# Four buffers for the feature-major context and a one-pair-at-a-time order on TensorE in a cross-attention layer

## What is computed

```
x = x + _L2_xattn_ref(_layernorm(x, axis=-1), ctx_1024, ctx_1024, mask_BxSxS2_ff0, Wq, Wk, Wv)

def _L2_xattn_ref(x1, x2, x3, mask, Wq, Wk, Wv):
    q = einsum('bsd,hd->bsh', x1, Wq)        # 8 x 64 x 256
    k = einsum('bsd,hd->bsh', x2, Wk)        # 8 x 1601 x 256
    v = einsum('bsd,hd->bsh', x3, Wv)
    scores = einsum('bqh,bkh->bqk', q, k) / sqrt(256)
    weights = softmax(scores + mask, axis=-1)
    return einsum('bqk,bkh->bqh', weights, v)
```

## Time and profile before

| | us |
|---|---|
| median of 3 runs | 3238.86 (3234.41 to 3239.84) |
| the profiled execution, its own time | 3242.19 |
| span of the profiled execution | 3240.4 |
| TensorE busy / VectorE busy / ScalarE busy | 2822.7 / 1634.3 / 1088.7 |
| this layer's first instruction, start | 2382.4 |
| first and last `scores`, start | 2397.8 and 2480.7 |
| last `mix`, start | 2502.8 |
| next layer's first instruction, start | 2519.4 |

### The profile page before, as it was taken

One profiled execution on the slowest core, in us unless ns is written; L12 is line 12 of the kernel. 1 busy time (PEld: TensorE's weight loads), 2 busy tenths in 40 slices (PEclk: granted clock), 3 DMA queues, 4 the chain that ended last, 5 costly groups with the idle time before them and its releaser, 6 DMA issues. The chain is left out here.

```text
span 3240.4 us, 43628 instructions
## 1 busy us (share of the span) xinstructions
PE 2822.7 (87%) x17456; PEld 1910.0 (59%) x17456; DVE 1634.3 (50%) x3626; ACT 1088.7 (34%) x1925; POOL 522.3 (16%) x280
## 2 busy tenths in 40 slices
PE   5899999999999998789999779989955789588776
PEld 2566666666666665446565536657932559477644
DVE  5556565665646454445555357754520520355463
ACT  2333333333333331135555446622311613111120
POOL 2012020211202000000000007731010320243200
PEclk8899999999999999889999989999977889799888
DMA  4123323232322210311000001126856158332101
GB/s 139 45 53 73 69 55 66 54 66 54 66 59 61 54 44 23 145 45 42 21 21 22 1 16 40 43 84 243 301 191 203 50 193 306 131 122 82 32 1 33
DMA packets 92096, 271.40 MB, mean 84 GB/s; under 512 B 7920, under 2 KB 57096, under 8 KB 85240
## 3 DMA queue, kind: packets, MB, share of 16 engines
q1 hardware_dynamic: 87896, 259.65, 26.6%
q0 software_dynamic: 2976, 8.13, 0.7%
q10 hardware_dynamic: 1024, 0.86, 0.1%
HBM read 256.64 MB, written 11.44 MB: 83 GB/s over the span
## 5 line engine op out<-in xcount | busy, mean ns | idle before, releaser
L1375 PE MATMUL L_xattn_bank<-L_xattn_keys_tok,L_xattn_probsT 119*128 119x257 f32 (+1 forms) x1792 | 452.7, 393 | 9.3 <-ACT L_xattn_probsT L1211 0.4
L1312 PE MATMUL L_xattn_wide<-L_xattn_keys_feat,weights_a 128*128 128x512 f32 (+2 forms) x1024 | 386.4, 521 | 1.3 <-DVE L_xattn_k_rnorm L1024 0.7
L1375 PEld LDWEIGHTS L_xattn_bank<-L_xattn_keys_tok,L_xattn_probsT 119*128 119x128 f32 (+1 forms) x1792 | 320.9, 190 | 96.5 <-issue 33.1
L1312 PEld LDWEIGHTS L_xattn_wide<-L_xattn_keys_feat,weights_a 128*128 128x128 f32 x1024 | 192.0, 193 | 153.8 <-issue 127.7
L1020 DVE COPY L_xattn_k_normed<-L_xattn_wide 128x833 f32<-128x833 f32 (+1 forms) x128 | 131.3, 1026 | 231.2 <-PE L_xattn_wide L1312 231.2
L2315 DVE TENSOR_TENSOR_SCAN L_attn_state<-L_attn_decay,L_attn_banks 128x1024 f32<-128x1024 f32 x80 | 182.7, 2286 | 69.6 <-PE L_attn_banks L2518 61.6
L1590 DVE CUSTOM_DVE_ANT_0 L_xattn_scores<-L_xattn_banks,L_xattn_mask 128x512 f32<-128x512 f32 (+1 forms) x256 | 131.4, 570 | 151.8 <-issue 151.8
L2421 POOL TENSOR_TENSOR L_attn_state<-L_attn_state,L_attn_C_rows 128x1024 f32<-128x1024 f32 x80 | 188.7, 2360 | 70.3 <-DVE L_attn_state L2315 70.2
L1126 POOL TENSOR_TENSOR L_xattn_keys_tok<-L_xattn_keys_tok,weights_a 119x1792 f32<-119x1792 f32 (+2 forms) x24 | 61.1, 2546 | 856.1 <-DVE L_xattn_keys_tok L965 856.1
L1205 ACT ACTIVATE L_xattn_scores<-L_xattn_scores,L_xattn_neg_max 128x833 f32<-128x833 f32 x128 | 119.6, 982 | 208.6 <-DVE L_xattn_neg_max L1045 208.6
L2518 PEld LDWEIGHTS L_attn_banks<-L_attn_B_diagonal,L_attn_dt_u_tok 128*128 128x128 f32 x1280 | 150.4, 193 | 66.3 <-issue 64.7
(11 more groups left out here) (504 smaller groups left out, 4562.6 us busy)
## 6 DMA issues: line engine op xcount, KB each, us to landing
L_xattn_k_scale<-L_xattn_k_scale_rows SPq DMA_DIRECT2D x128, 417.0 KB, 5.1
L_xattn_ctx_feat<-in_ctx_feat SPq DMA_DIRECT2D x24, 1601.0 KB, 10.0
L_ffn_expert_w<-in_x_L_ffn SPq DMA_DIRECT2D x16, 2056.0 KB, 8.0
L_ffn_expert_w<-in_x_L_ffn SPq DMA_DIRECT2D x15, 1028.0 KB, 6.2
L_ffn_expert_w<-in_x_L_ffn SPq DMA_DIRECT2D x15, 1024.0 KB, 5.2
L_attn_C_rows<-L_attn_c_rows SPq DMA_DIRECT2D x48, 256.0 KB, 3.2
L_xattn_ctx_tok<-in_ctx_tok SPq DMA_DIRECT2D x8, 1536.0 KB
L_xattn_ctx_tok_and_one<-in_ctx_tok SPq DMA_DIRECT2D x8, 1536.0 KB
```

What stands on the lines that cost most here:

```text
L1312: last = nc.tensor.matmul(wide[:, 2 * h + c, 0:n], wk[:, k, p * P:(p + 1) * P], xnT[b % 2][:, k, a:a + n], start=(k == 0), stop=(k == KT - 1))
L1375: last = nc.tensor.matmul(bS[:, 0:D + 1], pT[0:r, c, a, :, :].rearrange("p h q -> p (h q)"), xn[b % 2][0:r, t, :], start=(i == 0), stop=(i ...
```

## The change

Three edits, all in `l2_xattn`. The features get four buffers instead of three (`FEAT = 4`), and the waits of their loads are counted by four; the tokens stay at three. TensorE finishes a pair before it scores the next, and between `scores(u)` and `turn_weights(u)` it issues four matmuls of `keep_busy` into bank 4. VectorE's order is turned to match.

```diff
     RING = 3
+    FEAT = 4
...
-        cT = [sb("ctx_feat_%d" % n, [P, KT, CTX]) for n in range(RING)]
+        cT = [sb("ctx_feat_%d" % n, [P, KT, CTX]) for n in range(FEAT)]
...
-                        if b >= RING:
-                            sp.wait_ge(scored, (b - RING) // 2 + 1)
-                        sp.dma_start(cT[b % RING][:, :, :], L.aps["ctx_feat"][b].rearrange("(k p) n -> p k n", p=P)
-                                     ).then_inc(cT_loaded[b % RING], 16)
+                        if b >= FEAT:
+                            sp.wait_ge(scored, (b - FEAT) // 2 + 1)
+                        sp.dma_start(cT[b % FEAT][:, :, :], L.aps["ctx_feat"][b].rearrange("(k p) n -> p k n", p=P)
+                                     ).then_inc(cT_loaded[b % FEAT], 16)
...
                 scores_taken(0)
                 for u in range(PAIRS):
+                    divide(u)
+                    keep_result(u)
                     if u + 1 < PAIRS:
                         scores_taken(u + 1)
-                    divide(u)
-                    keep_result(u)
...
-                        pe.wait_ge(cT_loaded[b % RING], 16 * (b // RING) + 16)
+                        pe.wait_ge(cT_loaded[b % FEAT], 16 * (b // FEAT) + 16)
...
-                scores(0)
                 for u in range(PAIRS):
-                    if u + 1 < PAIRS:
-                        scores(u + 1)
+                    scores(u)
+                    keep_busy(L, ps[:, 4, :], 4)
                     turn_weights(u)
                     mix(u)
                     turn_mixed(u)
```

More of the change, by code:

```diff
@@ L579, in l2_xattn @@
         q_ready = sem("q_ready")
-        cT_loaded = [sem("ctx_feat_loaded_%d" % n) for n in range(RING)]
+        cT_loaded = [sem("ctx_feat_loaded_%d" % n) for n in range(FEAT)]
         ck_loaded = [sem("ctx_tok_loaded_%d" % n) for n in range(RING)]
@@ L714, in scores @@
                                 last = nc.tensor.matmul(ps[j * S:(j + 1) * S, c, 0:n], q2T[:, k, b * S:(b + 1) * S],
-                                                        cT[b % RING][:, k, a:a + n], start=(k == 0), stop=(k == KT - 1),
+                                                        cT[b % FEAT][:, k, a:a + n], start=(k == 0), stop=(k == KT - 1),
                                                         tile_position=(0, j * S))
```

## The result

The changed kernel takes 3217.6 us (median of 4 runs, 3216.6 to 3219.7) against 3239.4 for the kernel before. The ratio is 0.9937, 95% interval 0.9919 to 0.9954: 22 us or 0.7% faster, where 30 us were forecast.

The account below looks back on a forecast made before the run. The layer was taken as bound by a DMA stream with three holes: -27.85 (gaps) - 0.9 (bursts) - 1.4 (clock) = -30.1 us, taking the profiled 3242.2 to 3212.1; median forecast 3209 us, forecast-only range 3203 to 3215, whole range 3202 to 3220.

Parts of the forecast that it names:

- the partly cold chain: Rival: each pair 2 to 4 us over the DMA's time, scores 8.1 us, fillers at low clock; 3214 to 3221; chance 10%.
- The bound and the mechanism: In the layer, loads wait for token buffers that mix frees only after the next pair's scores, so the DMA runs dry.
- The three gaps of 27.85 us: Empty DMA stretches of 9.75, 9.55 and 8.55 us between load bursts; all were to close, -27.85 us.
- the rival of completion out of order: Tokens land only with their burst's end, so mix stays behind it; gain about 5 us, 3234; chance 7%.
- that of SP's issue: Rival: each token load needs 12 us of SP's issue, 26.1 us a pair; about -13.5 us, 3225; chance 6%.
- Buffers: A fourth feature buffer costs no time, lets features 4 and 5 follow at once, buys nothing while tokens are blocked.
- Start and end of a burst, -0.9 us: Later load bursts begin slowly; at 340 GB/s, with the last tokens, they save 0 to 1.8 us, half taken.
- The features of batch 7 at 2461.4: Last pair's features were to land 15.0 us into their burst, letting its scores end at 2467.0 or 2468.5.
- The clock, -1.4 us: In the last pair, mix was to gain 0 to 2.3 us because TensorE hardly stands still before it.
- fillers at the low clock: Four filler matmuls at 1.2 GHz take 7.5 us and delay the transposes by 3.3 us.
- The slower case: Rival: TensorE at 1.2 GHz throughout becomes the bound, 35 us a pair; layer 27 us longer, 3266; chance 3%.
- The rate of the loads: Loads of the later bursts at 358 GB/s would make the burst term -4.2 us; the forecast kept the trace's rates.

## Why the prediction was right, and where it was off

**The time.** The measured 3217.6 us lie 8.6 above the 3209 forecast, and outside the range that was given for the forecast alone, 3203 to 3215. They lie in the whole range, 3202 to 3220, because that also took in the partly cold chain. What the runs show for the difference is below, and it is mostly not that rival's mechanism.

**The bound and the mechanism: right.** The three gaps of 27.85 us closed, SP never waited for `mix`, and the loads ended 93.6 us after the layer's start where the forecast had 91.7. `mix(0)` ended at 33.2 us after the start of the layer (2407.50 + 5.83 - 2380.12), as forecast (2415.5 - 2382.4 = 33.1). So the tokens landed ahead of the features behind them, and the rival of completion out of order has fallen. So has that of SP's issue: the longest issue of tokens took 14.98 us, and the DMA share over the whole stream was 1.03.

**Buffers: right for the time, less so for their use.** They cost and bring nothing by themselves. But the prediction said that the fourth lets features 4 and 5 follow at once; with three, SP waited only 1.1 us in all.

**Start and end of a burst, -0.9 us: wrong in sign.** Without this term the loads would have ended 120.4 - 27.85 = 92.6 us after the layer's start, and with it at 91.7; they ended at 93.6. So the stream took 1.0 us more instead of 0.9 less, 1.9 us off. I took the rate of the first burst, 340 GB/s, as that of an endless one. In its first 43 us the new stream did have 342 GB/s, but over the 94 us the mean was 324.

**The features of batch 7 at 2461.4 (79.0 us after the layer's start): the step that failed.** The scores of pair 3 started at 85.4, so 6.4 us late. Of these, 1.9 us are the stream: the fifteenth completion came at 80.9. The other 4.4 us are the last completion. I had carried the landing time of 15.0 us into a burst over from bursts that began with all DMA engines idle. In this stream they do not finish together, and the run with the wide mask shows that the narrow masks have a part in it: without them the lag is 0.4 us there. Why the same masks left only 0.3 us in the kernel before is not shown.

**The clock, -1.4 us: right for `mix`, missing for `scores`.** The last `mix` did take 5.83 us instead of 8.1, a gain of 2.3. But I looked for the drop ahead of `mix`. For `scores` the prediction allowed 5.6 to 7.1 us (2461.4 to 2467.0 or 2468.5) and put no cost on it, since the last tokens were to come later. The late features made a wait of 2.3 us there, the clock fell, and `scores(3)` took 8.3 us instead of 5.6, or 2.7 us more; the run with fillers in that wait shows it. The prediction also said that at most some 3 us of a chain are at the low clock. Its own row has more: from 2416.96 to the first microsecond at 0.94, 2422 to 2423, is 5 us, and what is 2.5 us is their cost (8.14 us instead of 5.60).

The forecast for the layer was 137.0 - 30.1 = 106.9 us, and it took 114.5. With 6.4 us for the late features, 2.7 for `scores` and 0.9 back on `mix` (2.3 against the 1.4 counted), this would be 8.2 us late. The forecast also had a wait of up to 0.9 us between the transposes (2473.2) and the last tokens (2474.1), which is no longer there: 106.9 + 8.2 - 0.9 = 114.2, 0.3 us from what was measured.

**The rivals.** The time and the slow `scores` are those of the partly cold chain, to which I gave 10%: it asked for `scores` of 8.1 us and a time of 3214 to 3221. But it is only in part what happened. Its other sign, fillers at the low clock, did not come; they took 3.70 us each time. And in it the chain outlasts the loads in every pair, while here TensorE waited 2.3 to 3.0 us for features ahead of each pair, so the slow `scores` cost 2.7 us once, in the last pair. That the time fell into its range is in good part the 6.4 us of late features, which no rival had. The slower case was far off: in every pair the clock was back before `scores` ended.

**The rate of the loads.** The Trainium skill ("DMA: Bandwidth & Descriptors", Where 436 GB/s comes from) gives some 358 GB/s as what binds a core's loads from HBM, and the prediction set it against the 416 GB/s of the earlier trace rows. It did not bind here either: with the wide mask the stream held a mean of 371 GB/s for 82 us. What held the changed kernel's stream down to 324 was the 213 to 217 GB/s of the stretches with narrow masks.

## What to carry to other kernels

When a wait closes a circle (the loads wait for a buffer that the engine frees only after it has waited for the loads), move the work that frees the buffer ahead, or add a buffer to the ring that blocks (here shown only together with longer token rows and the wide mask), not to the one that starves. Once the stream is unbroken, look at its slowest completion and at the shape of each load: small loads that cover half of the partitions, 11% of the bytes, cost 16 us of 114, of which 9 were the stream, 4 the last completion and 3 the clock behind it. Such an edit is worth what the path makes of it: the same one line gave 2.6 us in the old order. And a filler paid only where the wait was already there and the work behind it was on the path; with no wait to fill, three groups cost 6.6 us.

## What the runs showed of the hardware that I had not expected

- A load into 64 partitions keeps all DMA engines busy (share 1.04) at 213 to 217 GB/s; into 128 partitions packets of the same size take 0.25 us instead of 0.49.
- The 16 completions of one load can spread: in the changed kernel, with narrow loads in the stream, the last came up to 4.4 us behind the fifteenth, and with the wide mask at most 1.1 us. In the kernel before it was 0.3 us, with narrow loads too, and for features 3 ahead of any gap.
- TensorE's clock went from 2.4 to 1.2 GHz within a wait of 2.3 us. After waits of 1.0 and 1.6 us it was still up, and so it was after the 2.07 us ahead of the last `scores` in the run with four token buffers (5.60 us). After the wait of 4.3 us in the run without fillers it was up at first and fell when TensorE had gone back to work (0.64 in 2404 to 2408). So the length of the wait alone does not tell.
- Token runs of 12 KB instead of 1 KB brought the end of all loads from 82.4 to 77.5 us after the layer's start. Reading every twelfth column made a pair's transposes 2.28 us instead of 2.09, up to the start of `mix`; a pair took 19.0 us with it, 18.8 to 19.7 without.
